# Cross-attention and expert layer on one core: the half tile moved to the middle, queries stacked in 128 rows, and the attention output divided before one shared projection

## The reference, cut to what matters

```
x = x + xattn(layernorm(x), ctx, Wq, Wk, Wv, Wo, bo)
    q, k, v = x @ Wq, ctx @ Wk, ctx @ Wv            # 16 heads of 64
    out     = softmax(q k^T / 8) v                  # per head
    result  = concat(out) @ Wo + bo
x = x + ffn(layernorm(x))    # routed experts and shared expert
```

## Time and profile before

| what | us |
|---|---|
| median of 3 runs | 3225.25 (3224.87 to 3225.56) |
| the profiled execution, its own time | 3223.51 |
| its span, first to last instruction | 3221.7 |
| granted TensorE clock, mean | 0.997 of full |
| TensorE busy | 3179.9 |
| VectorE busy | 2389.6 |
| ScalarE busy | 2017.8 |
| GpSimd busy | 1333.2 |

### The profile page before, as it was taken

The page is one execution under the profiler, slowest core; times in us unless marked ns, Lnnn a source line. Parts: engine busy times, 40 slices in busy tenths (PEclk is TensorE's granted clock), DMA queues, the critical chain, the costliest instruction groups (busy, mean ns, idle before and its releaser), DMA issues.

```text
span 3221.7 us, 40836 instructions
## 1 busy us (share of the span) xinstructions
PE 3179.9 (99%) x15118; PEld 2534.7 (79%) x15118; DVE 2389.6 (74%) x4882; ACT 2017.8 (63%) x2356; POOL 1333.2 (41%) x894
## 2 busy tenths in 40 slices
PE   7999999999999999999999999999999999999999
PEld 5777777778777777778777777777877778777787
DVE  5777777777777777777777777777777777777766
ACT  4666666666666666666666666666666666676555
POOL 5333443334333343334443344333433334225566
PEclk8999999999999999999999999999999999999999
DMA  2000000000000000000000000000000000105553
GB/s 82 1 17 1 17 1 1 18 1 18 1 18 1 18 1 1 17 1 18 1 18 1 18 1 18 1 1 18 1 18 1 18 1 1 40 3 122 120 129 76
DMA packets 31707, 67.48 MB, mean 21 GB/s; under 512 B 8339, under 2 KB 9620, under 8 KB 31124
## 3 DMA queue, kind: packets, MB, share of 16 engines
q1 hardware_dynamic: 31508, 64.88, 7.8%
HBM read 61.72 MB, written 2.62 MB: 20 GB/s over the span
## 4 chain that ended last, share of the span: by engine, by line
PE 96%; DVE 1%; POOL 1%; issue 1%; ACT 0%; DMA 0%; POOLq 0%; SPq 0%; DVEq 0%; ACTq 0%
PE st L593 12%; PE st L596 12%; PE side L535 11%; PE op L606 11%; PE op L612 11%; PE st L599 11%; PE op L609 11%; PE side L629 3%; PE st L716 2%; PE st L718 2%; PE st L717 2%; PE side L528 1%; PE op L620 1%; PE op L623 1%; PE side L530 1%; PE side L529 1%
## 5 line engine op out<-in xcount | busy, mean ns | idle before, releaser
L473 POOL TENSOR_TENSOR p_lo<-p_full,p_hi 128x1024 fp32r<-128x1024 f32 x320 | 819.7, 2562 | 1753.1 <-ACT p_hi L877 1753.1
L1156 DVE TENSOR_REDUCE m_part<-side 128x1 f32<-128x400 f32 x2016 | 1072.7, 568 | 502.3 <-PE side L535 502.2
L874 ACT ACTIVATE p_full<-st 128x1024 f32<-128x1024 f32 x768 | 788.8, 1027 | 876.8 <-PE st L599 848.5
L877 ACT ACTIVATE p_hi<-st 128x1024 fp32r<-128x1024 f32 x768 | 784.9, 1022 | 0.0
L1139 DVE TENSOR_TENSOR p_lo<-p_full,p_hi 128x1024 fp32r<-128x1024 f32 x448 | 545.5, 1218 | 85.6 <-ACT p_hi L877 85.6
L535 PE MATMUL side<-cT_hi,qT_hi 96*128 96x400 f32 x2016 | 554.5, 346 | 0.0
L593 PE MATMUL st<-qT_hi,cT_hi 97*128 97x512 f32 x1664 | 540.8, 406 | 11.9 <-DMA qT_hi<-m_row 11.1
L596 PE MATMUL st<-qT_lo,cT_hi 96*128 96x512 f32 x1664 | 524.3, 396 | 0.0
L606 PE MATMUL op<-p_hi,v_hi 128*97 128x512 f32 x1536 | 487.6, 398 | 1.6 <-DVE p_lo L1139 1.6
L612 PE MATMUL op<-p_hi,v_lo 128*97 128x512 f32 x1536 | 480.4, 394 | 0.0
L609 PE MATMUL op<-p_lo,v_hi 128*97 128x512 f32 x1536 | 480.4, 394 | 0.0
(11 more groups left out here) (171 smaller groups left out, 3072.1 us busy)
## 6 DMA issues: line engine op xcount, KB each, us to landing
w_rep<-w_rows SPq DMA_DIRECT2D x64, 512.0 KB, 6.6
keys_nat<-in_ctx_keys SPq DMA_DIRECT2D x16, 672.0 KB, 6.0
keys_tur<-in_ctx_turned SPq DMA_DIRECT2D x16, 600.4 KB, 4.8
gud_raw<-in_moe_w SPq DMA_DIRECT2D x2, 1152.0 KB, 7.7
out_x<-x SPq DMA_DIRECT2D x8, 256.0 KB, 2.0
x<-in_x SPq DMA_DIRECT2D x1, 1920.0 KB, 12.7
qT_hi<-m_row SPq DMA_DIRECT2D x64, 4.0 KB
oT<-e_row SPq DMA_DIRECT2D x64, 4.0 KB
```

Source lines behind the costliest of these rows:

```text
L473: pool.tensor_tensor(p_lo[:, slot(s), :], p_full[:, s % 2, :], p_hi[:, slot(s), :].bitcast(F32), ALU.subtract).then_inc(s_lo_pool, 1)
L874: act.activation(p_full[0:m, s % 2, :], made, ACT.Exp, scale=SCALE)
L877: act.activation(p_hi[0:m, slot(s), :], made, ACT.Exp, scale=SCALE).then_inc(s_ex, 1)
L1156: dve.tensor_reduce(m_part[:, k % NT, k // NT:k // NT + 1], where[:, 0:MAXW], AX.X, ALU.max).then_inc(s_drain, 1)
```

## The change

- The half tile is step 6 (`HALF`), steps 7 to 12 are tiles 6 to 11. `st` and `p_full` alternate by n + s, through the groups.
- Queries are stacked: three blocks of 128 rows in place of four of 96, the fourth head's in the lower 32 rows of the three. Q makes blocks 0 and 1, then block 2; copies take them apart again (three and two per job).
- Y is gone. ScalarE keeps the outputs with their denominators; SP sends these to `den` (8 x 128); VectorE adds the last key's part and inverts them after the side jobs of step 4; SP stores them to DRAM and spreads them over 96 partitions (`r_rep`). At step 10 VectorE multiplies (one operation of 768 columns, three of 256 on 32 partitions), ScalarE keeps the high part ahead of exp(11), VectorE the low part after lo(10), and Z, ahead of the weighing in step 12, projects all four heads in nine matmuls of 256 columns. VectorE sums Z over a batch in `y_sum`; V (i = 1, step 3) turns the sum, and VectorE adds it to x.
- B is kept stacked in high and low parts, which GpSimd makes in groups 0 and 1; the sum over its heads is four reductions and an addition.
- The place of M, T, U, V and the layer norm and routing steps is changed; deviations are made after step 11; the last group's output and routing are in the second and third chunk.

```
-        PLACES = {2: ("MM", "M"), 3: ("MM", "M"), 4: ("MM", "MM"), 5: ("MM", "M"), 6: ("MM", "MM"),
-                  7: ("MM", "MM"), 8: ("MM", "MY"), 9: ("MM", "MM"), 10: ("MM", "MM"), 11: ("YY", "YT"),
-                  12: ("QQ", "")}
-        EXTRA = {1: {5: "U"}, 2: {5: "L", 3: "N"}, 3: {5: "R"}}
+        PLACES = {2: ("MM", "M"), 3: ("MM", "M"), 4: ("MM", "MM"), 5: ("MM", "M"), 6: ("MM", "M"),
+                  7: ("MM", "MM"), 8: ("MM", "MM"), 9: ("MM", "MM"), 10: ("MM", "MM"), 11: ("", "T"),
+                  12: ("Z", "Q", "Q")}
+        EXTRA = {1: {3: "V", 5: "U"}, 2: {5: "L", 3: "N"}, 3: {5: "R"}}
...
+            def send_denominators(g):
+                sp.wait_ge(s_oe, g + 1)
+                sp.dma_start(den[:, :], oT[DC:OW, :].rearrange("o (a b) -> o a b", b=P)).then_inc(s_dl, 16)
+
+            def spread_inverted(g):
+
+                sp.wait_ge(s_rc, 2 * g + 2)
+                sp.dma_start(r_rows[g % 2].rearrange("(a b) -> a b", b=P), den[:, :]).then_inc(s_rd, 16)
+                sp.wait_ge(s_rd, 16 * (g + 1))
+                sp.wait_ge(s_on, g)
+                sp.dma_start(r_rep[:, :], r_rows[g % 2:g % 2 + 1, :].to_broadcast([DC, GQ])).then_inc(s_rr, 16)
...
             def body(b, i, g):
+                if g:
+                    send_denominators(g - 1)
+                    spread_inverted(g - 1)
...
+                    send_max_row(jobs_at(g)["T"][0] + 1, (i + 1) % 2)
                     if i == NGB - 1 and b >= 2:
                         store_routing(b - 2)
-                    send_max_row(jobs_at(g)["T"][0] + 1, (i + 1) % 2)
-                send_last_row(g)
...
             def project_queries(where, g, half, k):
-                for h in range(2):
-                    head = g * GH + 2 * k + h
-                    o = where[0:DC, h * NQ:(h + 1) * NQ]
...
+                for block in ((0, 1), (2,))[k]:
+                    o = where[:, block % 2 * NQ:(block % 2 + 1) * NQ]
+                    pe.matmul(o, A_hi[:, g, block, :], x_hi[:, half, :], start=True, stop=False)
+                    pe.matmul(o, A_hi[:, g, block, :], x_lo[:, half, :], start=False, stop=False)
+                    mm = pe.matmul(o, A_lo[:, g, block, :], x_hi[:, half, :], start=False, stop=True)
...
+            def project_outputs(where, g):
+
+                pe.wait_ge(s_ol, g + 1)
...
+                for k in range(3):
+                    pe.matmul(where[:, 0:NQ], B_hi[:, i, k, :], o_hi[:, k, :], start=(k == 0), stop=False)
+                    pe.matmul(where[:, 0:NQ], B_lo[:, i, k, :], o_hi[:, k, :], start=False, stop=False)
+                    mm = pe.matmul(where[:, 0:NQ], B_hi[:, i, k, :], o_lo[:, k, :], start=False, stop=(k == 2))
...
+                side_jobs(at[S - 1][2])
                 pe.wait_ge(s_ml, 16 * (g + 2))
-                pe.wait_ge(s_sum, g + 1)
+                pe.wait_ge(s_ex, n + (S - 1))
...
+                    if s == HALF:
+                        low_half()
+                    if s == S - 2 and g:
+                        divided_hi(g - 1, jobs_at(g - 1)["Z"][0] + 1 if g > 1 else 0)
                     exp(s)
...
+            def invert_denominators(g):
+
+                dve.wait_ge(s_dl, 16 * (g + 1))
+                dve.wait_ge(s_el, g + 1)
+                dve.tensor_tensor(den[:, :], den[:, :], e_row[:, g % 2, :], ALU.add).then_inc(s_rc, 1)
+                dve.wait_ge(s_rc, 2 * g + 1)
+                dve.reciprocal(den[:, :], den[:, :]).then_inc(s_rc, 1)
+
+            def divide_first(g):
+
+                dve.wait_ge(s_rr, 16 * (g + 1))
+                dve.tensor_tensor(o_all[0:DC, :, :].rearrange("p k t -> p (k t)"), oT[0:DC, 0:3 * NQ],
+                                  r_rep[:, 0:3 * NQ], ALU.mult)
+
+            def divide_last(g):
+
+                for k in range(3):
+                    third = slice(k * DT, (k + 1) * DT)
+                    ins = dve.tensor_tensor(o_all[DC:P, k, :], oT[third, 3 * NQ:GQ], r_rep[third, 3 * NQ:GQ], ALU.mult)
+                ins.then_inc(s_on, 1)
+
+            def divided_lo(g):
+                dve.wait_ge(s_oh, g + 1)
+                dve.tensor_tensor(o_lo[:, :, :], o_all[:, :, :], o_hi[:, :, :].bitcast(F32),
+                                  ALU.subtract).then_inc(s_ol, 1)
...
                 for t in range(2, S):
                     if t == S - 1:
+                        side_jobs(at[t][0])
+                        lo(t - 1)
+                        lo(t)
+                    elif t == HALF:
+                        side_jobs(at[t][0])
+                        lo(t - 1)
                         sum_half()
-                        side_jobs(at[t][0])
-                        early_steps()
-                        lo(t)
                     elif t == S - 2:
                         lo(t - 1)
+                        if g:
+                            divided_lo(g - 1)
                         side_jobs(at[t][0])
+                    elif t == S - 3 and g:
+                        side_jobs(at[t][0])
+                        divide_first(g - 1)
+                        divide_last(g - 1)
                     else:
                         side_jobs(at[t][0])
                         lo(t - 1)
                     side_jobs(at[t][1])
+                    if g and t == 4:
+                        invert_denominators(g - 1)
+                    if i == 1 and t == S - 2:
+                        batch_stats()
+                    elif g and t == S - 2:
+                        late_steps(g - 1)
...
-                    dve.tensor_reduce(B_sum[0:DC, :], B_all[0:DC, :, 0:D].rearrange("p h d -> p d h"), AX.X,
-                                      ALU.add).then_inc(s_bs, 1)
+                    link(dve.tensor_reduce(B_sum[0:DC, :], B_raw[0:DC, :, :, :].rearrange("p i k d -> p d (i k)"), AX.X,
+                                           ALU.add))
+                    for k in range(3):
+                        ins = dve.tensor_reduce(B_rest[k * DT:(k + 1) * DT, :],
+                                                B_raw[DC:P, :, k, :].rearrange("p i d -> p d i"), AX.X, ALU.add)
+                    link(ins)
+                    dve.tensor_tensor(B_sum[0:DC, :], B_sum[0:DC, :], B_rest[:, :], ALU.add).then_inc(s_bs, 1)
```

More of the change, by code:

```diff
@@ L360, in _ @@
                         store_output(c - 1)
[L361 removed]
+                if c == 2:
                     store_routing(B - 2)
@@ L587, in _, with scores @@
             turn_maxima(bank(J0_T))
[L589 to L590 removed]
+            def scores(n, s, slot, par):
+                tile = tile_of(s)
+                keys = slice(tile * P, tile * P + P)
                 halves = [slice(j * BANK, (j + 1) * BANK) for j in range(2)]
+                into = st[:, (n + s) % 2]
                 for j in range(2):
[L593 to L594 removed]
+                    pe.matmul(into[:, j, :], cT_hi[par][:, keys], qT_hi[slot][:, halves[j]], start=True, stop=False)
                 for j in range(2):
[L596 to L599 removed]
+                    mm = pe.matmul(into[:, j, :], cT_hi[par][0:DC, keys], qT_lo[slot][:, halves[j]],
+                                   start=False, stop=(s == HALF))
+                for j in range(0 if s == HALF else 2):
+                    mm = pe.matmul(into[:, j, :], cT_lo[par][:, keys], qT_hi[slot][0:DC, halves[j]],
                                    start=False, stop=True)
@@ L798, in queries_hi @@
                 act.wait_ge(s_fill, filled)
-                act.activation(qT_hi[slot][0:DC, k * BANK:(k + 1) * BANK], where[0:DC, :], ACT.Copy).then_inc(s_qh, 1)
-            def products(banks, cols):
-                return banks[:, :, cols].rearrange("p j (c m) -> p j c m", c=2)
-            def four_heads(tile, n):
-                return tile[:, 4 * n:4 * n + 4, :].rearrange("p (c j) m -> p j c m", c=2)
+                for into, made in unstacked(qT_hi[slot], where, k):
+                    ins = act.activation(into, made, ACT.Copy)
+                ins.then_inc(s_qh, 1)
             def keep_products(n, banks):
@@ L817, in _ @@
             act.wait_ge(s_ab, 2)
-            act.activation(four_heads(A_hi, 0), products(op, slice(0, 2 * DC)), ACT.Copy).then_inc(s_xh, 1)
+            for into, made in stacked(A_hi, 0, op):
+                ins = act.activation(into, made, ACT.Copy)
+            ins.then_inc(s_xh, 1)
             act.wait_ge(s_tur, 16)
@@ L1000, in queries_lo @@
                 dve.wait_ge(s_qh, count)
-                cols = slice(k * BANK, (k + 1) * BANK)
-                dve.tensor_tensor(qT_lo[slot][:, cols], where[0:DC, :], qT_hi[slot][0:DC, cols].bitcast(F32),
-                                  ALU.subtract).then_inc(s_drain, 1)
+                high = unstacked(qT_hi[slot], where, k)
+                for (into, made), (kept, _) in zip(unstacked(qT_lo[slot], where, k), high):
+                    ins = dve.tensor_tensor(into, made, kept.bitcast(F32), ALU.subtract)
+                ins.then_inc(s_drain, 1)
             def combine_max():
@@ L1100, in _ @@
```

(8 more changed lines are left out.)

373 lines of the change are left out of this document (212 added, 161 removed).

## The result

The changed kernel takes 3268.05 us (median of 4 runs, 3266.79 to 3268.84) against 3225.4 for the kernel before beside it: ratio 1.0133, 95% interval 1.012 to 1.0145. It is slower by 1.3%. The forecast of 3215 missed by 53 us, the sign is wrong, and the result lies 6 us above the range.

A forecast was written before the change was run, and what follows sets the result against it. TensorE, busy 99% of the span, was taken as the bound. From 3223.5 us, savings and small costs gave 3149.4; new waits of 15.1 and 49.0 made 3213.5 profiled, 3215 for the median; range 3160 to 3262.

The forecast's parts named there:

- terms 1 to 3: TensorE: Z in place of Y, -46.1 us; nine Q matmuls for twelve, -21.9; Q's wait for Y's drain gone, -11.2.
- the term that decides: Steps 4 to 6: denominators' sum and reciprocal delay VectorE's maxima; step 6 waits 0.79 us on average, 62 groups, +49.0.
- Step 10 to Z: After step 10's divisions on VectorE, Z waits 0.24 us for the quotient's low part; 63 times, +15.1 us.
- with 0.08 of overlap each: Step 10: VectorE's four multiplications each overlap by 0.08 us, 1.95 us in all, ending at 619.74.
- if each multiplication took no overlap it is 0.5: Step 10: without overlap between the multiplications, Z's wait is 0.5 us in place of 0.24; bounds of the term 0 to 32.
- B_sum's term: First group's end: the sum of B takes 6.5 us where it took 3.92, +2.5 us.
- the start and the expert stage: Some fourteen more small copies and subtractions before the first scores, and projection steps in the second chunk: +2 us, between 0 and 6.
- the 2.9 that was to go: Last group: its wait of 2.93 us for the half tile goes, as the half is now the seventh step; -2.9 us.
- Case C: GpSimd's lo(5) starts before VectorE's lo(4) and holds it off; step 6 waits 3.1 us; 3250 to near 3285, chance 0.28.

The follow-up runs named there:

- the ninth run: The changed kernel with its half tile last again, as step 12, its sum behind Z's, all else left: 3441.2 us, 173 more.
- the fourth run: The changed kernel with the reciprocal of the denominators issued twice, 0.94 us more on VectorE at the end of step 4: 3558.6 us, 290 more.

## Why the prediction was wrong

**TensorE's terms were right.** Y to Z, Q and Q's wait (terms 1 to 3) with V make -1.20 a group. The steps give -1.29 without the waits; the other 0.08 is step 9, where the kernel before lost that much behind step 8's Y. The run with repeated matmuls confirms Q's price directly (20.5 against 21.9).

**Steps 4 to 6, "the term that decides", was right in mechanism and size**: 0.79 a group forecast, 0.70 measured; the reciprocal's 6.2 ns an element gave 0.95, the row 0.94. The estimate of 1.2 us from the repeat count of 8 that the Trainium skill gives (VectorE: DVE Perf Modes, "First, the fixed hardware budget") does not fit; the profile's slope held, and held down to 8 elements (0.20). The parts came out too: 0.47 for the sum and the reciprocal, 0.23 for the half tile.

**Step 10 to Z was the right wait with the wrong size**: 0.24 forecast, 0.61 measured, and T, of which I wrote that TensorE "has it", waits 0.15. The step that failed is "with 0.08 of overlap each". The changed kernel's chain:

```profile
633.94 1.05 DVE m_part L1268 x2
634.99 0.86 DVE o_all L1112
635.87 0.42 DVE o_all L1119
636.30 0.42 DVE o_all L1119
636.73 0.42 DVE o_all L1119
637.18 1.07 DVE m_part L1268 x2
638.46 0.51 DVE p_lo L1251
...
639.51 0.96 DVE o_lo L1124
```

The small divisions start 0.43 apart, with no overlap, and the pair of maxima begins only after the last of them (1.07, not 0.97). It is not that they are short: they begin in other partitions than the operation ahead (last section). The divisions end 0.28 later than walked, the maxima 0.40, and all that follows keeps the 0.40. I had priced that case ("if each multiplication took no overlap it is 0.5") and put it aside. It costs (0.61 + 0.15 - 0.24) x 62 = 32 us, the largest part of the miss. The mechanism, Z waiting for the row of divisions, was the forecast one; its term was mis-sized. The experiment that splits the divisions shows it.

**Step 8 was not walked at all**: 0.23 x 62 = 14 us. I followed the shift to step 6 and stopped there, though step 8's weighing is the half tile's now and as much shorter, and VectorE's low part of the half (1.22, as long as a whole tile's) stands in step 7 just ahead of the maxima it has to drain. With the half tile last, the ninth run, step 8 has no wait (3.52).

**The one-off terms were too small.** B_sum's term was forecast at +2.5, the start and the expert stage at +2 ("most lie beside maxima and matmuls"). Measured: the start 4.3, groups 0 and 1 8.7, the last group and the expert stage 5.5. For the start I counted copies and not the queues behind them: ScalarE's eleven small copies for each block of products kept GpSimd's A_lo waiting 13.9, and the context's shift, the release of the second context and the first row of maxima stood behind it in turn. For group 1 I had left out that B's low part is 3.50 of GpSimd beside the first divisions, and that TensorE's clock falls behind its stalls there (3.4 us). Of the last 5.5, the expert stage's chunks 0 to 2 take 1.1 more, 1.4 less and 4.7 more than before, and the last group does not show the 2.9 that was to go, as its steps 8 and 9 take 4.1 each (before, 3.1 and 2.9). There the chain holds four subtractions of the expert weights on VectorE in a row (4.14 us from 2938.30) and then a low part that GpSimd's L521 holds off to 2.3. Some 1.8 of the 5.5 is again the lower clock. This was read and not tried: which of the placed steps costs what stays open.

In sum, the miss is 53.3 on the profiled execution (its own time 3266.8, forecast 3213.5): 32 for Z and T, 14 for step 8, -6 for steps 5 and 6, -5 for step 9, about 7 in groups 0 and 1 and about 11 for the start and the end.

**The rivals.** Case C was real as a mechanism, with its edge about where it was said to be (by the walk 0.18 us off in the first groups and 0.03 in the fourth, measured 0.3 to 0.5 and 0.07 to 0.09), but it did not happen: no lo was held to 3 us in the changed kernel (2.31 is the longest). That the time came out slower, as case C had it, is for other reasons. Its chance of 0.28 for "slower" was too small, since many small terms of one sign could also get there; the range had no room for them beside case C. The hold-off that the Trainium skill states (SBUF — State Buffer, "Who interferes with whom") is at work in three places here: the fourth run, the ninth, and group 1 of the changed kernel.

## What to carry to other kernels

Walk a delay forward until a gap on the delaying engine has absorbed it: the idle time must lie behind the delayed work and ahead of its user. A small operation over few partitions costs by elements per partition: a transfer into 128 x 8 was worth 30 us here. Where two engines exclude each other, write down which of them starts first and by how much; a margin of 0.3 us, in some groups of 0.1, hid a cost of 4.65 us a group. Price a long stall of TensorE with what follows it: here 1.8 of those 4.65 us were matmuls at the lower clock. And an operation that begins in other partitions than its neighbours is to be priced without overlap.

## What the runs showed of the hardware beyond what was expected

- Whether a VectorE operation starts 0.07 to 0.09 us before the one ahead ends goes here not with its length but with where its partitions begin. In the changed kernel the pairs of maxima do, and so do operations as short as 128 x 8 (L1161, 0.07), 128 x 128 (L1073, 0.08) and the sum of the half tile, which is on partitions 0 to 63 (L1257, 0.08). The three small divisions, written to partitions from 96 on and read from 0, 32 and 64, each start 0.01 after the end of the one ahead. So do the pieces of the queries taken apart (L1090), and the low part of the half tile, written to partitions from 64 on, starts 0.03 after, in every group. The maxima behind the divisions and behind that low part start 0.03 after too. An operation that needs the result of the one ahead also starts 0.03 after it, wherever it begins.
- Sixty-four partitions of 1024 elements take as long as 128 (1219 against 1218 ns).
- The sum of the same 1024 numbers takes 0.27 at the least as 8 x 128 (0.33 in the median, 0.46 in the mean, as GpSimd holds it off) and 0.15 as 128 x 8 (0.22 in the median); the reciprocal takes 0.94 and 0.20.
- A VectorE operation that GpSimd holds off ends after GpSimd's by nearly its own whole length: 1.08 us for 1024 elements a partition (alone 1.21), 0.82 for 768 (0.94; in group 1 135.56 against 134.74), 0.42 for 384 (0.55), 0.05 to 0.09 for 32 and 64 (0.24 and 0.23). How far in the other one was makes no difference: the 62 low parts of the fourth run began 0.27 to 0.77 us after GpSimd's, and all ended 1.07 to 1.08 after it.
- Behind stalls of TensorE its granted clock fell to the lower level for some us: in every group of the fourth experiment (stalls of 1.7 to 2.5 us), in group 1 of the changed kernel (4.4 and 3.3) and behind the longest boundaries of the ninth run (1.8). It did not in the steady groups of the changed kernel, where TensorE stands idle for less than 0.5 at a time.
